# Hybrid block on one core: the first attention with 64-row score tiles, units of four pairs, decays from a 30-row matmul and no loop over batches

## The chip, the core and the metric

The kernel runs on one core of a Trainium2 chip, in one launch. The metric is the device time of that launch in microseconds (us). The engines are TensorE (PE; PEld is its weight load), VectorE (DVE), ScalarE (ACT), GpSimd (POOL) and SyncE (SP, which here only issues DMAs). Each runs its own instructions in order and waits on semaphores.

## The reference

Four layers stand behind one another, each behind a layernorm and with a residual: attention A, experts, a delta rule, experts. The change touches attention A alone, of which this is the core (8 batches B, T = 512 tokens, C = 128, 16 heads of 8):

```python
qkvgr = jnp.einsum('btc,oc->bto', x, W)
log_g = jax.nn.log_sigmoid(qkvgr[..., 3 * C:])
log_G = jnp.cumsum(log_g, axis=1).transpose(0, 2, 1)
S = jnp.einsum('bhtd,bhsd->bhts', Q, K)
Tm = DEG * jnp.log(jnp.abs(S) + EPS) + jnp.log(scale)      # DEG = 2
Z = Tm + log_G[..., :, None] - log_G[..., None, :]         # where s <= t
P = jnp.exp(Z - Z_rowmax)
y = (P @ V) / P.sum(-1)
```

So a weight is (|S| + eps)^2 times the decay exp(log_G[t] - log_G[s]), and the kernel computes it as that product, without the logarithm of S.

## The kernel before

Heads go in eight pairs p; a pair is 2Q + hf with Q in 0..3 and hf in 0..1. Tokens go in eight blocks of 64 (L = 64, index m). A batch is cut into 24 units (NU), 12 for each hf. Unit n has a key block m and the queries from block m on. For m < 4 it holds two pairs, for m >= 4 four pairs (`unit`, L134). Each unit goes through a line of engines:

- PE `scores` (L756): one matmul per pair. The weights `kf` are 128 rows by 128 columns with the two heads of the pair on the diagonal, 64 by 64 each, and zeros beside them. The moving operand is the bf16 feature tile `qf`. Rows are 48 products of three-part bf16 splits for each head.
- DVE `magnitude` (L577): the absolute value, from PSUM to SBUF.
- ACT `square` (L369): (|S| + eps)^2 into `pw`.
- POOL `diagonal` (L265): the diagonal block of the unit times `decay`, the masked decay inside a block.
- PE `attend` (L771): 64-column float32 matmuls with 18-column weights, one for each block and pair. The four Q write to four 32-partition groups of `pDia` and `pOff` and share the columns of the array.

PE is ahead by two units: at step n it issues `scores(n + 2)` and then `attend(n - 1)`. All engines run the same list of steps n = 0..23, with the preparation of the next batch put between the units at fixed n: TURN (transposes of the normalized x, n = 4), QK (projection, 6), the splits into bf16 parts (DVE, 8 and 10), VALUES (10), SUMS (15), DECAY (16 to 23, one m at each), EXPAND (18 and 20). `turn_back` and `finish` at n = 1 and 3 close the batch before.

The features go through HBM: SP writes the bf16 parts to `parts_scratch` by six DMAs (L168), waits for them, and loads `kc` (L173) and `qf` (L175), 1 MB each. DVE `expand` (L564) copies `kc` into the two diagonal halves of `kf`. For the decays POOL `ramps` (L237) makes tri times the log gate for each m, and PE `decay_sums` (L741) multiplies it by the 128-row float32 matrix `after` and adds the mask `never` by a bf16 matmul; ACT `decays` (L361) takes the exponential.

Batch 0 and the last batch are written out; batches 1 to 6 are a loop of three rounds on every engine (`Fori`, L187, L290, L426, L675, L852). Ahead of batch 0 stands a prologue: scaling of the weights with a guard from a POOL reduction (L231), the moments of all eight batches, and the preparation of batch 0.

## Time and profile before

| what | us |
|---|---|
| median of 3 runs | 1322.86 (1318.02 to 1323.44) |
| the profiled execution | 1334.64 |
| its span, first to last instruction | 1332.8 |
| attention A: start of the span to the last DVE instruction of the layer | about 502 |
| prologue: up to the first `attend` | 73.4 |
| batches 0 to 6, `attend` of one to that of the next | 391.8 in all |
| last batch to the last transpose | about 35 |

A row of a timeline begins with its start and its length in us. For PE a row is one group of like instructions; a float32 matmul of the program counts as two instructions. In brackets stands the idle time ahead of it and what ended it. The first `attend` of a batch begins with rows of L790 (the zero matmuls that start the accumulation), so these mark the batches: there are four such rows in each, two at n = 1 and 2, and two at n = 13 and 14.

### The profile page before, as it was taken

How to read it: one execution, taken by the hardware profiler on the slowest of the kernel's cores; microseconds unless marked ns; L12 is line 12 of the kernel's file. 1: busy time of each engine (PE TensorE's matmuls, PEld its weight loads, DVE VectorE, ACT ScalarE, POOL GpSimd, SP SyncE). 2: the span in 40 equal slices, each digit the busy share in tenths (PEclk: the TensorE clock that was granted, in tenths of full speed). 3: DMA queues.
4: the chain of work that ended last, by engine and by line, in shares of the span. 5: the costliest groups of instructions: out<-in, count | busy, mean ns of one | idle time of the engine just before them, and what ended most of it. 6: DMA issues, size and time to landing. Idle time of an engine off the chain costs nothing. (4 is left out here: it accounts for less than half of the span.)

```text
span 1332.8 us, 25209 instructions
## 1 busy us (share of the span) xinstructions
PE 912.9 (68%) x8236; PEld 629.3 (47%) x8236; DVE 793.4 (60%) x1615; ACT 551.8 (41%) x1205; POOL 578.7 (43%) x659
## 2 busy tenths in 40 slices
PE   0678878788787785029982958984676773507993
PEld 0355544545455462017771328734555563206772
DVE  6366676667676676202226129999999999501223
ACT  1465756566475652014431631015555541103441
POOL 3347467273655731444441000007777780172442
PEclk9989999899999996559995969996889887758997
DMA  2312303033040304036642680000001001016665
GB/s 69 126 65 65 128 3 128 18 112 112 19 128 7 122 3 192 32 96 181 185 137 76 205 205 1 1 0 0 0 0 63 16 16 32 9 52 164 183 188 166
DMA packets 129403, 110.08 MB, mean 83 GB/s; under 512 B 21984, under 2 KB 115104, under 8 KB 128928
## 3 DMA queue, kind: packets, MB, share of 16 engines
q1 hardware_dynamic: 123760, 98.08, 25.4%
q0 software_dynamic: 5120, 10.53, 2.4%
q8 instruction: 64, 1.05, 0.3%
q14 instruction: 27, 0.22, 0.1%
q10 hardware_dynamic: 432, 0.20, 0.1%
HBM read 64.01 MB, written 44.65 MB: 82 GB/s over the span
## 5 line engine op out<-in xcount | busy, mean ns | idle before, releaser
L583 DVE TENSOR_SCALAR a_mag<-a_pS 128x1024 int32<-128x1024 int32 (+1 forms) x192 | 182.1, 955 | 130.5 <-PE a_pS L767 128.7
L271 POOL TENSOR_TENSOR a_pw<-a_pw,a_decay 128x128 f32<-128x128 f32 (+1 forms) x192 | 121.3, 635 | 185.6 <-ACT a_pw L375 184.7
L375 ACT ACTIVATE a_pw<-a_mag,a_eps_a 128x1024 f32<-128x1024 f32 (+1 forms) x192 | 173.7, 928 | 64.7 <-DVE a_mag L583 63.8
L1053 POOL DMA_INDIRECT ys_dram<-f_yo,f_who x96 | 91.9, 957 | 139.3 <-DVE f_yo L1253 120.6
L1241 DVE TENSOR_SCALAR f_ysT<-f_bY,f_b2s 128x256 f32<-128x256 f32 x48 | 23.2, 484 | 175.1 <-PE f_bY L1341 147.3
L795 PE MATMUL a_pOff<-a_pw,a_vo 128*18 128x64 f32 x3584 | 126.5, 225 | 0.0
L1600 POOL TENSOR_TENSOR d_pb_p<-d_Q,d_s_sb 128x512 f32<-128x512 f32 x32 | 37.3, 1167 | 198.1 <-ACT d_s_sb L1700 198.1
L767 PE MATMUL a_pS<-a_qf,a_kf 128*128 128x128 bf16 (+7 forms) x512 | 98.4, 295 | 10.4 <-issue 6.8
L795 PEld LDWEIGHTS a_pOff<-a_pw,a_vo 128*18 128x18 f32 x3584 | 104.8, 102 | 0.0
L1096 ACT ACTIVATE f_hs<-f_bH,f_b1s 128x256 f32<-128x256 f32 x192 | 75.2, 474 | 67.1 <-issue 37.6
L1045 POOL DMA_INDIRECT xs_dram<-f_xa,f_pos x64 | 61.7, 964 | 94.0 <-DVE f_pos L1226 75.1
L2073 PE MATMUL d_c<-d_pb_p,d_ident 128*128 128x256 f32 x256 | 72.0, 450 | 43.4 <-POOL d_pb_p L1606 43.4
L1321 PE MATMUL f_bA<-ident,f_xs 128*128 128x128 f32 x96 | 21.6, 309 | 113.7 <-DMA f_xs<-xs_dram 62.8
L1331 PE MATMUL f_bH<-f_xsT,f_w1s 128*128 128x256 f32 x384 | 95.8, 394 | 0.0
L1341 PE MATMUL f_bY<-f_hs,f_w2s 128*128 128x256 f32 x384 | 90.8, 379 | 0.0
L243 POOL TENSOR_TENSOR a_ramp<-a_tri,a_logg 128x512 f32<-128x512 f32 x64 | 69.5, 1088 | 38.4 <-DVE a_logg L530 31.0
L2073 PEld LDWEIGHTS d_c<-d_pb_p,d_ident 128*128 128x128 f32 x256 | 58.2, 231 | 57.6 <-issue 42.2
L1087 ACT ACTIVATE f_xsT<-f_bA 128x256 f32<-128x256 f32 x48 | 18.4, 384 | 151.8 <-PE f_bA L1321 145.9
L750 PE MATMUL a_M<-a_ramp,a_after 128*128 128x512 f32 x128 | 73.8, 659 | 7.4 <-POOL a_ramp L243 6.8
L2073 PE MATMUL d_c<-d_pb_d,d_ident 128*128 128x256 f32 (+1 forms) x256 | 63.3, 413 | 22.0 <-POOL d_pb_d L1606 22.0
L1331 PEld LDWEIGHTS f_bH<-f_xsT,f_w1s 128*128 128x128 f32 x384 | 72.0, 197 | 9.6 <-issue 0.6
L792 PE MATMUL a_pDia<-a_pw,a_vd 128*18 128x64 f32 x1024 | 58.5, 228 | 25.0 <-POOL a_pw L271 24.4
(333 smaller groups left out, 1897.3 us busy)
## 6 DMA issues: line engine op xcount, KB each, us to landing
parts_scratch<-a_parts SPq DMA_DIRECT2D x32, 384.0 KB, 4.0
f_w1s<-in_L_ffn_w_dram SPq DMA_DIRECT2D x48, 256.0 KB
f_w2s<-in_L_ffn_w_dram SPq DMA_DIRECT2D x48, 256.0 KB
a_kc<-parts_scratch SPq DMA_DIRECT2D x8, 1024.0 KB, 6.0
a_qf<-parts_scratch SPq DMA_DIRECT2D x8, 1024.0 KB, 9.0
xs_dram<-blank SPq DMA_DIRECT2D x12, 516.0 KB, 5.3
f_xs<-xs_dram SPq DMA_DIRECT2D x48, 129.0 KB, 2.2
parts_scratch<-a_parts SPq DMA_DIRECT2D x16, 256.0 KB, 4.0
```

Of the source, the lines that this page charges most:

```text
L243: pool.tensor_tensor(ramp[:, m % 2, :, :], tri[:, :].unsqueeze(1).broadcast_to([P, NP, L]), logg[:, 0:64].rearrange("p (a m) -> p a m", m= ...
L271: pool.tensor_tensor(own, own, decay[:, k, m, pairs_of(hf, qs), :], ALU.mult)\
L375: act.activation(pw[:, n % 4, 0:N], mag[:, n % 3, 0:N], ACT.Square, bias=eps_a[:, 0:1])\
L583: dve.tensor_scalar(mag[:, n % 3, 0:2 * N].bitcast(I32).rearrange("p (l t) -> p l t", l=2), pS[:, 2 * (n % 2):2 * (n % 2) + 2, 0:N].bitcas ...
L750: pe.matmul(M[:, :], after[:, :], ramp[:, m % 2, :, :].rearrange("p a t -> p (a t)"), start=True, stop=False)
L767: ins = pe.matmul(pS[:, 2 * (n % 2) + l // half, at:at + width(m)], kf[:, k, p, m, :, :].rearrange("p x t -> p (x t)"), qf[:, k, p, L * m: ...
L795: ins = pe.matmul(pOff[lo:hi, L * i:L * i + L], vo[:, vo_at(m, i), p, :], wi, start=False, stop=(m == NM - 2), skip_group_check=True)
L1053: pool.indirect_dma_start(ys_dram[f][:, :], bass.IndirectOffsetOnAxis(ap=who[:, q, a:a + 1], axis=0), yo[:, q, a, :], None).then_inc(ys_ou ...
L1096: ins = act.activation(hs[:, q % 2, n, :], bH[:, 2 * (q % 2) + n // 2, ST * (n % 2):ST * (n % 2) + ST], ACT.Gelu, bias=b1s[:, q, n:n + 1])
L1331: ins = pe.matmul(bH[:, 2 * (q % 2) + n // 2, ST * (n % 2):ST * (n % 2) + ST], w1s[:, q, P * n:P * n + P], xsT[:, q % 2, :], start=True, s ...
L1341: ins = pe.matmul(bY[:, 0:ST], w2s[:, q, n, :], hs[:, q % 2, n, :], start=(n == 0), stop=(n == NF - 1))
L2073: ins = pe.matmul((c5, c6)[a][:, 0:64 * chunks].rearrange("p (c x) -> p c x", x=64), ident[:, :], po[:, k], start=(k == 0), stop=(k == 15))
```

## The change

Units: all 24 hold four pairs. For m < 4 the queries are cut in two instead of the pairs: a unit with the diagonal and one without (`BLOCKS`). The column counts of a unit are 4, 4, 4, 3, 3, 3, 3, 2, 4, 3, 2, 1 blocks of 64 for each pair.

Scores: each pair has two matmuls of 64 rows by 64 columns, one for each head, at rows and columns 0 to 63 and 64 to 127. `kf` is loaded directly in the form of `kc`, and `expand` and the zeros are gone. 64 score matmuls of a batch become 192.

Diagonals: POOL multiplies only in the 16 units of a batch that have a diagonal; `attend` of the other eight waits for ACT's `square` alone.

Decays: the ramps are gone. One more matmul at SUMS gives the cumulated log gates with the heads on partitions; DVE splits them in three bf16 parts (`cum_split`, n = 16); SP's `cumulated` writes them to HBM in two layouts, waits, and loads them into `here` and `there` (30 rows, with constants 1 and -1 in the other rows). A bf16 matmul of 30 rows gives a decay block. The eight decays of the next batch are done two at a time at n = 20 to 23.

The order: `Fori` is replaced by a Python loop on all engines. TURN 4 to 5, QK 6 to 7, VALUES 10 to 9 (with the second half of it behind the scores of n = 10), DECAY 16 to 20, `normalize` one batch earlier at n = 20, `finish` ahead of `magnitude`.

ACT: the natural logarithm and the exponential come from one table set, loaded once in the prologue.

Prologue: the moments of batch 0 alone are ahead of its normalization, those of batches 1 to 7 stand behind its splits; the guard's maximum goes over PE instead of POOL's reduction.

```diff
-        def width(m):
-            return T - L * m
+        BLOCKS = [part for m in range(NM) for part in
+                  ([(m, m, m + 4 - m // 2), (m, m + 4 - m // 2, NM)] if m < NM // 2 else [(m, m, NM)])]
         def unit(n):
             hf, r = divmod(n, HU)
-            if r < NM:
-                return hf, r // 2, (2 * (r % 2), 2 * (r % 2) + 1)
-            return hf, r - NM // 2, (0, 1, 2, 3)
+            return (hf,) + BLOCKS[r]
+        def on_diagonal(n):
+            return unit(n)[1] == unit(n)[2]
+        ND = sum(on_diagonal(n) for n in range(NU))
+        def diagonals(n):
+            return sum(on_diagonal(i) for i in range(n + 1))
...
-        TURN, QK, VALUES, SUMS, DECAY, EXPAND = 4, 6, 10, 15, 16, 18
+        TURN, QK, VALUES, SUMS, DECAY = 5, 7, 9, 15, 20
         FIN = (1, 3)
+        def decay_pair(n):
+            return (2 * n, 2 * n + 1) if 0 <= n < NM // 2 else ()
...
-                sp.wait_ge(s["kx_done"], 2 * bb)
-                sp.dma_start(kc[:, :, :], scratch[k, 1].rearrange("(p r) c t -> (r c) p t", p=NP))\
...
+            def cumulated(bb):
+                sp.wait_ge(s["cum_split"], 4 * bb + 4)
+                sp.wait_ge(s["cum_in"], 32 * bb)
+                sp.dma_start(cums[0].rearrange("q a m c -> (a m) q c"), cum3[:, :, :]).then_inc(s["cum_out"], 16)
+                sp.dma_start(cums[1].rearrange("q a m c -> q (a m c)").rearrange("q (x a m t) -> (a m) q x t", x=2, a=NP, m=NM),
+                             cum3[:, :, :].rearrange("p q (x t) -> p q x t", x=2)).then_inc(s["cum_out"], 16)
+                sp.wait_ge(s["cum_out"], 32 * bb + 32)
+                sp.wait_ge(s["decay_ps"], NM * bb)
+                sp.dma_start(here[6:KC, :, :], cums[0].rearrange("q a m c -> (q a) m c")).then_inc(s["cum_in"], 16)
+                sp.dma_start(there[0:6, :, :, :].rearrange("r a m t -> r (a m t)"),
+                             cums[1].rearrange("q a m c -> q (a m c)").rearrange("q (x f) -> (q x) f", x=2))\
+                    .then_inc(s["cum_in"], 16)
             features(0, 0)
+            sp.wait_ge(s["consts"], 2)
+            cumulated(0)
...
+                    cumulated(b + 1)
...
-            with sp.Fori(1, B - 2, 2) as b:
+            for b in range(1, B - 2, 2):
...
-            pool.wait_ge(s["guard_step"], 2)
-            pool.partition_all_reduce(wmx[:, :], wss[:, :], P, RMAX).then_inc(s["guard_step"], 1)
-            pool.wait_ge(s["guard_step"], 3)
-            for k in range(2):
-                pool.memset(kf[:, k, :, :, :, :].rearrange("p a m x t -> p (a m x t)").bitcast(F32), 0.0)\
-                    .then_inc(s["kf_zero"], 1)
-            def ramps(bb, m, first=False):
-                pool.wait_ge(s["logg_done"], bb + 1)
-                if not (first and m < 2):
-                    pool.wait_ge(s["decay_ps"], NM * bb + m - 1)
-                pool.tensor_tensor(ramp[:, m % 2, :, :],
-                                   tri[:, :].unsqueeze(1).broadcast_to([P, NP, L]),
-                                   logg[:, 0:64].rearrange("p (a m) -> p a m", m=NM)[:, :, m:m + 1]
-                                   .broadcast_to([P, NP, L]), ALU.mult).then_inc(s["ramp_done"], 1)
+            step(pool.memset(here[:, :, :], 0.0))
+            step(pool.memset(there[:, :, :, :], 0.0))
+            for q in range(3):
+                step(pool.affine_select(out=here[:, :, :].rearrange("p m (x t) -> p m x t", x=2),
+                                        in_=here[:, :, :].rearrange("p m (x t) -> p m x t", x=2),
+                                        compare_op=ALU.not_equal, fill=1.0, base=-2 * q,
+                                        pattern=[[0, NM], [-1, 2], [0, L]], channel_multiplier=1))
+                step(pool.affine_select(out=there[:, :, :, :].rearrange("p a m t -> p a (m t)"),
+                                        in_=there[:, :, :, :].rearrange("p a m t -> p a (m t)"),
+                                        compare_op=ALU.not_equal, fill=-1.0, base=-6 - NP * q,
+                                        pattern=[[-1, NP], [0, NM * L]], channel_multiplier=1))
+            pool.wait_ge(s["c_step"], st)
+            pool.sem_inc(s["consts"], 1)
...
-                    diagonal(b, n, k)
+                    if on_diagonal(n):
+                        diagonal(b, n, k)
...
+                    for m in decay_pair(n - DECAY - 1):
+                        decays(b + 1, 1 - k, m)
...
+            act.preload_act_table_set("natural_log_exp_and_others")
...
+            def cum_split(bb):
+                dve.wait_ge(s["cum_ps"], bb + 1)
+                dve.wait_ge(s["cum_out"], 32 * bb)
+                dve.tensor_copy(cum3[:, 0, :], M0[0:64, 192:320]).then_inc(s["cum_split"], 1)
+                dve.wait_ge(s["cum_split"], 4 * bb + 1)
+                dve.tensor_tensor(cum_r[:, :], M0[0:64, 192:320], cum3[:, 0, :], ALU.subtract)\
+                    .then_inc(s["cum_split"], 1)
+                dve.wait_ge(s["cum_split"], 4 * bb + 2)
+                dve.tensor_copy(cum3[:, 1, :], cum_r[:, :]).then_inc(s["cum_split"], 1)
+                dve.wait_ge(s["cum_split"], 4 * bb + 3)
+                dve.tensor_tensor(cum3[:, 2, :], cum_r[:, :], cum3[:, 1, :], ALU.subtract)\
+                    .then_inc(s["cum_split"], 1)
...
-            def expand(bb, k, par, first=False):
-                dve.wait_ge(s["feat_k"], 16 * bb + 16)
-                if first:
-                    dve.wait_ge(s["kf_zero"], 2)
-                else:
-                    dve.wait_ge(s["s_ps"], NU * (bb - 1))
-                lo, hi = L * par, L * par + L
-                dve.tensor_copy(kf[lo:hi, k, :, :, par, :].rearrange("p a m t -> p (a m) t"),
-                                kc[lo:hi, :, :].rearrange("p a (m t) -> p (a m) t", t=L))\
-                    .then_inc(s["kx_done"], 1)
...
+            dve.wait_ge(s["x_in"], 16 * (B - 1))
+            moments(1, B, 2 * TT)
             gate_prep(0)
+            rstds(1, B, 6)
...
+                    if n == 20 and b + 2 < B:
+                        normalize(b + 2)
+                    if n == QK + 1:
                         split_rest(b + 1, 0)
...
+            pe.wait_ge(s["guard_step"], 2)
+            pe.transpose(M1[0:2, 0:P], wss[:, :], ident[:, :]).then_inc(s["guard_step"], 1)
+            pe.wait_ge(s["guard_step"], 5)
+            pe.matmul(M1[:, P:P + 2], ones2[:, :], wmx2[:, :], start=True, stop=True).then_inc(s["guard_step"], 1)
...
+                pe.matmul(M0[0:64, 192:320], logg[:, 0:64], upto[:, :], start=True, stop=True)\
                     .then_inc(s["cum_ps"], 1)
             def decay_sums(bb, m):
-                pe.wait_ge(s["ramp_done"], NM * bb + m + 1)
+                pe.wait_ge(s["cum_in"], 32 * bb + 32)
                 if m >= 2:
                     pe.wait_ge(s["decay_sb"], NM * bb + m - 1)
                 if m == 1:
@@ -747,44 +791,49 @@
                     pe.wait_ge(s["cum_sb"], 6 * bb + 2)
                     pe.wait_ge(s["tok_ps"], bb + 1)
                 M = (M1, M0)[m % 2]
-                pe.matmul(M[:, :], after[:, :], ramp[:, m % 2, :, :].rearrange("p a t -> p (a t)"),
+                pe.matmul(M[:, :].rearrange("p (a t) -> p a t", t=L), here[:, m, :], there[:, :, m, :],
...
-                for l, Q in enumerate(qs):
+                for Q in range(4):
                     p = 2 * Q + hf
-                    half = len(qs) // 2
-                    at = width(m) * (l % half)
-                    ins = pe.matmul(pS[:, 2 * (n % 2) + l // half, at:at + width(m)], kf[:, k, p, m, :, :].rearrange("p x t -> p (x t)"),
-                                    qf[:, k, p, L * m:T], start=True, stop=True)
+                    at = L * (end - first) * (Q % 2)
+                    for par in range(2):
+                        lo, hi = L * par, L * par + L
+                        ins = pe.matmul(pS[lo:hi, 2 * (n % 2) + Q // 2, at:at + L * (end - first)],
+                                        kf[lo:hi, k, p, L * m:L * m + L], qf[lo:hi, k, p, L * first:L * end],
+                                        start=True, stop=True)
...
+                if first == m:
+                    pe.wait_ge(s["pdg_done"], ND * b + diagonals(n))
+                else:
+                    pe.wait_ge(s["sq_done"], NU * b + n + 1 + AHEAD_MAG)
...
+                        for m in decay_pair(n - DECAY):
+                            decay_sums(b + 1, m)
```

How the order moves at three places. First PE, around n = 19 to 21 of batch 0 before; `a_M` is the PSUM tile of the decays, `a_pS` that of the scores:

```order
L750 MATMUL a_M<-a_ramp,a_after 128x512
L752 MATMUL a_M<-a_never,a_ident_b 128x512
L767 MATMUL a_pS<-a_qf,a_kf 128x192 x4
L792 MATMUL a_pDia<-a_pw,a_vd 18x64 x2
L795 MATMUL a_pOff<-a_pw,a_vo 18x64 x8
L750 MATMUL a_M<-a_ramp,a_after 128x512
L752 MATMUL a_M<-a_never,a_ident_b 128x512
L767 MATMUL a_pS<-a_qf,a_kf 128x128 x4
L792 MATMUL a_pDia<-a_pw,a_vd 18x64 x2
L795 MATMUL a_pOff<-a_pw,a_vo 18x64 x8
```

The same steps of PE in the changed kernel:

```order
L812 MATMUL a_pS<-a_qf,a_kf 64x192 x8
L841 MATMUL a_pDia<-a_pw,a_vd 18x64 x4
L844 MATMUL a_pOff<-a_pw,a_vo 18x64 x8
L794 MATMUL a_M<-a_there,a_here 128x512
L796 MATMUL a_M<-a_never,a_ident_b 128x512
L794 MATMUL a_M<-a_there,a_here 128x512
L796 MATMUL a_M<-a_never,a_ident_b 128x512
L812 MATMUL a_pS<-a_qf,a_kf 64x128 x8
L844 MATMUL a_pOff<-a_pw,a_vo 18x64 x8
```

A decay stood in each step from n = 16 on; now two stand in each step from n = 20 on, ahead of that step's scores, and they read what SP's last two DMAs bring.

Second SP, the transfers of one batch before:

```order
L168 DMA parts_scratch<-a_parts 128x3x512 x2
L168 DMA parts_scratch<-a_parts 128x2x512
L168 DMA parts_scratch<-a_parts 128x3x512 x2
L168 DMA parts_scratch<-a_parts 128x2x512
L173 DMA a_kc<-parts_scratch 128x8x512
L175 DMA a_qf<-parts_scratch 128x8x512
```

And in the changed kernel:

```order
L180 DMA parts_scratch<-a_parts 128x3x512 x2
L180 DMA parts_scratch<-a_parts 128x2x512
L180 DMA parts_scratch<-a_parts 128x3x512 x2
L180 DMA parts_scratch<-a_parts 128x2x512
L184 DMA a_kf<-parts_scratch 128x8x512
L186 DMA a_qf<-parts_scratch 128x8x512
L193 DMA cum_scratch<-a_cum 64x3x128
L194 DMA cum_scratch<-a_cum 64x6x64
L198 DMA a_here<-cum_scratch 24x1024
L199 DMA a_there<-cum_scratch 6x4096
```

Four DMAs are new, and they stand behind the two large loads on the same queue.

Third DVE in the prologue, between the guard and the splits of batch 0, before:

```order
L456 TENSOR_SCALAR a_wn<-a_wn,a_guard 128x128
L458 COPY a_wT<-a_M 128x384
...
L470 BN_STATS a_stats<-x 128x6 x32
L474 BN_AGGR a_mv<-a_stats 128x2 x32
...
L496 TENSOR_SCALAR a_xn<-x,a_mv,a_rstd 128x128 x4
L504 TENSOR_TENSOR a_rest<-a_M,a_parts 128x512 x2
L510 TENSOR_TENSOR a_parts<-a_rest,a_parts 128x512 x2
L517 COPY a_gates<-a_M 128x4x8 x2
```

And in the changed kernel, where four statistics stand ahead of the guard:

```order
L513 TENSOR_SCALAR a_wn<-a_wn,a_guard 128x128
L521 TENSOR_SCALAR a_xn<-x,a_mv,a_rstd 128x128 x4
L648 COPY a_wT<-a_M 128x384
...
L529 TENSOR_TENSOR a_rest<-a_M,a_parts 128x512 x2
L535 TENSOR_TENSOR a_parts<-a_rest,a_parts 128x512 x2
L473 BN_STATS a_stats<-x 128x6 x28
L476 BN_AGGR a_mv<-a_stats 128x2 x28
...
L542 COPY a_gates<-a_M 128x4x8 x2
```

28 of the 32 statistics have moved from ahead of the normalization to between the splits and the gates.

## Rows read from the trace of the kernel before

**Rows 1.** Windows: stretch, length, busy us of PE, PEld, DVE, ACT, POOL, then PEclk.

```profile
410.80:435.40 24.60, 19.50 (x385) 13.45 (x385) 20.22 (x37) 15.28 (x23) 6.88 (x12) 1.00 0.13 41
435.40:465.20 29.80, 25.14 (x366) 14.45 (x368) 19.05 (x22) 19.40 (x28) 24.64 (x27) 1.00 0.35 111
465.20:500.00 34.80, 30.58 (x673) 21.74 (x672) 25.82 (x38) 20.52 (x25) 12.59 (x23) 0.95 0.01 3
```

**Rows 2.** Timeline of PE, the marks of batches 0, 6 and 7.

```profile
73.39 0.41 PE L790 MATMUL a_pOff<-a_pw,a_zeros 128*18 128x64 f32 x4 [3.87 <-POOL a_pw L271]
...
410.78 0.30 PE L790 MATMUL a_pOff<-a_pw,a_zeros 128*18 128x64 f32 x4
...
435.40 0.30 PE L790 MATMUL a_pOff<-a_pw,a_zeros 128*18 128x64 f32 x4 [2.00 <-issue]
...
465.17 0.30 PE L790 MATMUL a_pOff<-a_pw,a_zeros 128*18 128x64 f32 x4
```

**Rows 3.** Timeline of SP in batch 6.

```profile
431.67 4.64 SPq L168 DMA_DIRECT2D parts_scratch<-a_parts  x6
440.91 0.36 SPq L173 DMA_DIRECT2D a_kc<-parts_scratch  x1
441.31 0.58 SPq L175 DMA_DIRECT2D a_qf<-parts_scratch  x1
```

**Rows 4.** DMA view: count, KB each, median us from issue to landing.

```profile
a_kc<-parts_scratch SPq DMA_DIRECT2D x8, 1024.0 KB, 6.0
a_qf<-parts_scratch SPq DMA_DIRECT2D x8, 1024.0 KB, 9.0
...
f_xs<-xs_dram SPq DMA_DIRECT2D x48, 129.0 KB, 2.2
...
fg_dram<-d_pb_p SPq DMA_DIRECT2D x16, 32.0 KB, 2.7
```

**Rows 5.** Timeline of PE at n = 20 of batch 6.

```profile
449.95 1.13 PE L750 MATMUL a_M<-a_ramp,a_after 128*128 128x512 f32 x2
450.91 0.38 PE L752 MATMUL a_M<-a_never,a_ident_b 128*128 128x512 bf16 x1
451.13 0.39 PE L767 MATMUL a_pS<-a_qf,a_kf 128*128 128x128 bf16 x4
```

**Rows 6.** Timeline of PE, a unit of four pairs and the row after a unit of two.

```profile
401.10 0.52 PE L795 MATMUL a_pOff<-a_pw,a_vo 128*18 128x64 f32 x24
...
411.91 0.50 PE L767 MATMUL a_pS<-a_qf,a_kf 128*128 128x384 bf16 x2
```

**Rows 7.** Lines by form, 70 to 530 us: count, busy us, mean ns, idle before.

```profile
L271 POOL TENSOR_TENSOR a_pw<-a_pw,a_decay 128x128 f32<-128x128 f32 x128 | 68.3, 535 | 150.2 <-ACT a_pw L375 150.2
...
L243 POOL TENSOR_TENSOR a_ramp<-a_tri,a_logg 128x512 f32<-128x512 f32 x56 | 59.1, 1056 | 5.3 <-PE a_M L752 5.0 <-DVE a_logg L530 0.3
...
L271 POOL TENSOR_TENSOR a_pw<-a_pw,a_decay 128x256 f32<-128x256 f32 x64 | 53.0, 835 | 35.4 <-ACT a_pw L375 34.5
...
L573 DVE COPY a_kf<-a_kc 64x4096 bf16<-64x4096 bf16 x14 | 34.6, 2475 | 0.4
...
L353 ACT ACT_TABLE_LOAD x7 | 9.0, 1283 | 2.7 <-DVE a_tail L538 2.7
...
L538 DVE TENSOR_TENSOR a_tail<-a_b_tot,a_M 128x64 f32<-128x64 f32 x7 | 1.6, 222 | 0.2
```

**Rows 8.** Timeline of PE behind the loop's first back edge.

```profile
237.25 0.92 PE L767 MATMUL a_pS<-a_qf,a_kf 128*128 128x448 bf16 x2 [3.52 <-issue]
```

**Rows 9.** Timeline of the prologue, DVE, PE and SP.

```profile
18.74 2.61 DVE L456 TENSOR_SCALAR a_wn<-a_wn,a_guard 128x128 f32<-128x128 f32 x1
...
23.59 6.28 DVE L470 BATCH_NORM_STATS2 a_stats<-x 128x6 f32<-128x128 f32 x32
...
35.04 1.09 PE L703 MATMUL a_M<-a_ident,a_xn 128*128 128x128 f32 x4 [12.45 <-DVE a_xn L496]
...
43.44 4.65 SPq L168 DMA_DIRECT2D parts_scratch<-a_parts  x6
```

241 lines of the change are left out of this document (122 added, 119 removed).

## The prediction

> **What bounds the kernel now.** I read the marks of the batches in PE's timeline first [rows 2], then the windows between them [rows 1], and last the single rows of PE, SP and the lines by form. The reader is to see three things. First, the layer before the first attend takes 73.4 us, batches 0 to 6 take 465.17 - 73.39 = 391.8 us or 55.97 each, and the last one about 35 [rows 1, 2]. Second, in a batch without a loop's edge (batch 6, 54.4 us) PE is busy 19.50 + 25.14 = 44.6 us and DVE 39.3; PE idles a sixth and is the bound, with short stops in which a unit waits for DVE or POOL [rows 1]. Third, the last batch, which prepares no next one, takes 35: the preparation costs some 20 us of a batch, and the change works mostly on that.
>
> For the DMA chain I cut batch 6 into three parts by its marks [rows 2, 3, 5]: A, from the mark at n = 1 to the first DMA of the features, 431.67 - 410.78 = 20.9 us; B, from there to the decay of n = 20, 449.95 - 431.67 = 18.3; C, from there to the next mark, 465.17 - 449.95 = 15.2.
>
> **The change part by part.**
>
> Attend. A unit of two pairs with m = 0 takes from 410.78 to 411.91, 1.13 us for 36 instructions or 31 ns each; one of four pairs has its 24 of L795 in 0.52, the tail included, or 22 ns [rows 2, 6]. The units of m < 4 have 432 instructions in a batch (416 of L792 and L795, 16 of L790). PE saves 432 x 9.5 ns = 4.1 us.
>
> Scores. Twelve units of a half hold 4, 5, 2 and 1 groups of 256, 192, 128 and 64 columns for each pair. Four full-row matmuls of 128 columns take 0.31 us in the order of the queue (451.13 to 451.44, its length 0.39) [rows 5]; that is 78 ns for one against 53 ns of columns. I take the two 64-row matmuls of a pair as side by side, since the four Q of an attend already are. Then the sum of scores stays at some 10 us a batch. Bounds: it falls by nothing, and it rises by 10 us if they follow one another.
>
> Decays. The float32 pass takes 450.91 - 449.95 = 0.96 us, the bf16 mask 0.22 [rows 5]. The new matmul is bf16 with as many columns as the mask, so 0.22: 8 x 0.74 = 5.9 us less for PE. The extra matmul at SUMS is under 0.3.
>
> PE goes from 44.6 to about 44.6 - 4.1 - 5.9 + 0.3 = 34.9 us.
>
> DVE loses the two expansions, 2 x 2.475 = 4.95, and gains four operations of a size like L538's 0.222, together 0.9 [rows 7]: 39.3 - 4.1 = 35.2. ACT loses two table loads of 1.283 [rows 7]: 34.7 - 2.6 = 32.1. POOL loses 8 x 1.056 of ramps, and 16 x 0.535 of diagonals become 8 x 0.835 (68.3 us against 53.4 over all batches): 31.5 - 8.4 - 1.9 = 21.2 [rows 1, 7].
>
> With PE and DVE at 35 and units that hand over two deep, I would give a batch 42 us if nothing else bound it: the 35 of DVE and some 7 where one of the two has a step and the other waits (batch 6 has 10 of 54).
>
> The new wait. PE's decays of n = 20 need `here` and `there`. Behind the waiting PE instruction stand the scores of n = 20 on, so DVE, ACT and POOL run dry. The chain, from the first feature DMA t0: the load of `kf` is issued at t0 + 9.24, that of `qf` 0.40 later [rows 3]. `kf` lands 6.0 after its issue and `qf` 9.0 after its own [rows 4], that is 3.4 us apart though issued 0.4 apart: the one waits for the other on the queue. `qf` lands at t0 + 9.64 + 9.0 = 18.6. The two small writes are issued at t0 + 10.3, but stand behind 2 MB on the same queue; I give them 1 us behind `qf`, 19.6. Then SP issues the two reads (0.4 each) and they land as a small load does, 2.2 [rows 4]: 22.5. The bounds of this: if the writes were not held back, they would land 2.7 after their issue [rows 4], and the whole would be t0 + 16; reads that share the engines with `qf` make 18.5 of it. If writes of 128 and 256 bytes a piece take 2 us more, 24.5. Without a wait PE would come to n = 20 about 13 us after t0 (nine units of 1.5, less the first). So B is set by the wait: 22.5, taken because the landing times of `kc` and `qf` are the nearest rows.
>
> A, after: DVE has in it its magnitudes, finish, splits and gates, which are now later by one step (n = 11 instead of 10) but without a wait for an old turn. DVE was busy 20.2 of 24.6 in the first half [rows 1]. I take 20 (18 to 22). C, after: PE has five units less 8 x 0.74 of work, but ACT has eight exponentials there in four units, and POOL the seven products of `vo`; part of those is done during the wait. PE comes out of an idle time of 22.5 - 13 = 9.5 us, and after the idle 3.5 of the loop's edge two matmuls of 448 columns took 0.92 us [rows 8]; their columns alone are 0.75 at 1.2 GHz and 0.37 at 2.4, so PE came back at the lower clock. Unslowed, C's PE work is some 9 us by the rows above (eight decays at 0.43, five groups of scores and of attends at 0.4 to 0.5, a turn back under 1), with ACT's exponentials beside it 10; I take 12 (10 to 15). A batch: 20 + 22.5 + 12 = 54.5, seven of them 381.5, against 391.8: -10.3. That includes the loop's edges: two in batches 2 and 4, 3.5 us each with a slow clock behind them [rows 8]. Code that is written out has to be fetched too; the written-out batches 0 and 7 show no such stop.
>
> Prologue. DVE no longer does all statistics ahead of the first transposes: 6.28 us and as much as is left to 35.04 [rows 9], and the guard no longer waits for POOL. The scaling of the weights took 2.61 us at 18.74, while POOL filled `kf`. The transposes start at 35.04. From 23.59 on lie 11.4 us of statistics, their deviations and the normalization, of which some 10 go; the scaling's 2.3 above its usual 0.3 go; and the guard, which began behind POOL's reduction and POOL's fill, comes an estimated 9 earlier: near 13.5. POOL now fills and selects `here` and `there` in the same stretch, 4096 elements a row like `kf`; if each of DVE's operations is held as that one was, it is 21. I take 17. From there to the first attend: 38.4 before; now 8.4 to the features' first DMA [rows 9], the 22.5 of the chain, eight decays that PE and ACT hand to each other at about 0.95, and 4 us for one unit's magnitude, square, diagonal and handovers (estimates): 42.5. So 59.5 instead of 73.4: -14 (-10 to -19).
>
> Last batch: two-pair units gone, 4.1 us of PE, of which DVE (25.8 of 34.8 busy) lets through some 3: -3.
>
> Sum: -14 - 10 - 3 = -27 against the profiled execution's 1334.64, whose span is 1332.8: 1307.6. The median of the runs is 11.8 lower than that execution: 1296.
>
> **The rivals.**
>
> The wait is shorter. The small writes pass the large loads, or land with them. For it: they are only 48 KB each and the write side is idle. Against: the two loads landed one after the other. B is 18.5, and C loses 1.5 since the idle time is short: 7 x -5.5 = -38.5, 1257.
>
> No wait at all. The units are slower than I think, or the chain is faster, so that n = 20 comes later. Then a batch is 42: 7 x -12.5 = -87.5, 1208. Against it: the old kernel itself reached n = 20 18.3 us after t0, 4 us before the 22.5.
>
> Slower: the clock. After each wait of 10 us PE runs at 1.2 GHz, and if it stays there through C and into A, because units with waits between them do not raise it again, C's 9 us of PE work doubles to 18, A becomes 21 and B, with the slow small writes, 24: 63 a batch, 7 x 8.5 = +59.5, 1355. It decides from 58.4 us a batch on, where 1323 is reached. For it: [rows 8]. Against: at 465 the clock is 0.95 over a batch with short stops [rows 1].
>
> The score halves follow one another. The two matmuls of a pair write two halves of one PSUM bank. If that holds the second back, scores double by 10 us a batch; 15 of 24 units lie outside B, and DVE covers a quarter: 7 x 4.8 = +33.6, 1330, at the edge of no change. Against: the four Q of attend write four groups of one bank and take 22 ns each [rows 6]. The Trainium skill, page TensorEngine Tiling (Array Packing), section Restrictions and Gotchas, says that different row tiles cannot use the same PSUM bank at once; attend's groups are column tiles, so no row here speaks against that rule. By it the time would be the 1330 of this paragraph.
>
> **How the numbers follow.** The forecast 0.45; wait shorter 0.20; no wait 0.10; the clock 0.13; the halves 0.12. The forecast's own range, from A, B, C and the prologue, is 1268 to 1322. For the whole I leave out most of no wait and the upper part of the clock: 1228 to 1336. A measurement here can tell about 0.5% from no change, 1316.2 to 1329.5. Faster: 0.42 of the forecast, 0.30 of the two shorter cases and 0.01 of the halves, 0.73. Same: 0.03 of the forecast, 0.06 of the halves, 0.02 of the clock, 0.11. Slower: 0.05 of the halves and 0.11 of the clock, 0.16.
>
> **What would show it.** In the changed profile: the row of L794 at n = 20 with several us of idle ahead of it, ended by a DMA into `here` or `there`; marks of the batches (L839) 54 us apart; a first mark near 60; L812 groups of 8 matmuls of 256 columns near 0.5 us, or near 1 if the halves follow one another; PE busy about 35 us in a batch; a granted clock under 0.95 in the stretches behind the wait. It would be wrong if the decays find their data in time, if the marks lie under 48 or over 59 us apart, or if the first mark is over 66.

## The result, and the profile after

The changed kernel is slower: a median of 1341.66 us against 1323.15 of the kernel before beside it, a ratio of 1.013 (95% interval 1.0078 to 1.0181). One of its runs was disturbed and is out of that ratio. The profiled execution took 1342.41 us with a span of 1340.6. The forecast was 1296, its range 1228 to 1336.

Where the time went, first by windows. These three answer to [rows 1]: batch 6 up to n = 13, from there to the next mark, and the last batch (same columns; PEclk is the seventh number, behind POOL's).

```profile
428.46:450.76 22.30, 17.32 (x449) 12.19 (x449) 18.64 (x33) 15.67 (x23) 5.82 (x8) 1.00 0.05 16
450.76:485.70 34.94, 25.00 (x422) 13.68 (x423) 14.99 (x25) 16.96 (x26) 13.98 (x15) 0.66 0.36 119
485.70:522.00 36.30, 25.09 (x776) 18.06 (x776) 28.72 (x51) 21.14 (x25) 12.20 (x19) 0.91 0.02 3
```

The first half of a batch is 2.3 us shorter, the second 5.1 longer, with the granted clock at 0.66 where it was 1.00. PE is busy 25.00 of the 34.94 us there, at that clock; DVE, ACT and POOL are busy under half.

The marks in PE's timeline answer to [rows 2].

```profile
69.48 0.31 PE L839 MATMUL a_pOff<-a_pw,a_zeros 128*18 128x64 f32 x7 [0.54 <-POOL a_pw L291]
...
428.46 0.31 PE L839 MATMUL a_pOff<-a_pw,a_zeros 128*18 128x64 f32 x7 [0.48 <-ACT a_off_sb L400]
...
450.76 0.44 PE L839 MATMUL a_pOff<-a_pw,a_zeros 128*18 128x64 f32 x8 [2.46 <-issue]
...
485.70 0.31 PE L839 MATMUL a_pOff<-a_pw,a_zeros 128*18 128x64 f32 x7 [0.48 <-ACT a_off_sb L400]
```

The prologue is 69.5 us (before 73.4), batches 0 to 6 are 485.70 - 69.48 = 416.2 (before 391.8), and the last one, to DVE's first instruction of the experts at 520.46, 34.8 (before 502.82 - 465.17 = 37.7). That is -3.9, +24.4 and -2.9, together +17.6; the medians say +18.5. The rest of the kernel has the same code; it took 820.1 us in this execution and 830.0 in the profiled one of before, which is why the two profiled executions differ by 7.8 only.

SP's timeline in batch 6 answers to [rows 3], the landing times to [rows 4].

```profile
449.01 4.47 SPq L180 DMA_DIRECT2D parts_scratch<-a_parts  x6
457.63 0.36 SPq L184 DMA_DIRECT2D a_kf<-parts_scratch  x1
458.03 0.58 SPq L186 DMA_DIRECT2D a_qf<-parts_scratch  x1
458.92 1.24 SPq L193 DMA_DIRECT2D cum_scratch<-a_cum  x1
460.19 0.88 SPq L194 DMA_DIRECT2D cum_scratch<-a_cum  x1
466.65 0.32 SPq L198 DMA_DIRECT2D a_here<-cum_scratch  x1
467.01 0.30 SPq L199 DMA_DIRECT2D a_there<-cum_scratch  x1
```

```profile
a_kf<-parts_scratch SPq DMA_DIRECT2D x8, 1024.0 KB, 6.1
a_qf<-parts_scratch SPq DMA_DIRECT2D x8, 1024.0 KB, 8.6
```

PE at n = 20 answers to [rows 5]:

```profile
469.56 0.60 PE L794 MATMUL a_M<-a_there,a_here 30*128 30x512 bf16 x1 [7.73 <-DMA a_there<-cum_scratch]
470.10 0.61 PE L796 MATMUL a_M<-a_never,a_ident_b 128*128 128x512 bf16 x1
470.64 0.60 PE L794 MATMUL a_M<-a_there,a_here 30*128 30x512 bf16 x1
```

The wait is there, 6.5 to 9.2 us in each batch. The matmuls of the decays behind it begin 0.54 us apart up to 481.3, where they are 0.32 apart at a clock of 1.00 (e13 below); eight decays and what stands between them fill C without a stop, up to the 0.48 ahead of the mark. The windows around the wait, in order of time:

```profile
454.11:460.94 6.83, 5.15 (x150) 3.56 (x149) 5.31 (x13) 3.28 (x5) 1.61 (x2) 1.00 0.48 159
460.94:461.83 0.89, 0.84 (x24) 0.59 (x24) 0.67 (x2) 0.52 (x1) 0.00 (x0) 0.50 1.06 377
461.83:469.56 7.73, 0.01 (x1) 0.00 (x0) 1.69 (x2) 2.08 (x3) 6.34 (x5) 0.50 0.58 189
469.56:481.42 11.86, 11.86 (x111) 4.46 (x111) 2.34 (x3) 5.40 (x9) 4.17 (x5) 0.50 0.01 1
```

Two things are to be seen. The clock fell 0.9 us before the long wait began, behind three short stops of PE (0.21, 0.59 and 0.93 us for DVE and POOL); it did so in batches 1, 3, 4 and 6, and at the beginning of the wait or within it in 5, 0 and 2. And it stayed at 0.50 for 11.86 us in which PE never stopped; in the seven batches it came back 10.6 to 18.2 us behind the wait. Cut by the marks as in the prediction, the means over seven batches are A 21.5, B 20.7, C 17.2, in all 59.5.

### The profile page after: what moved, and what is told of

It is laid out like the page before. It is cut to its first block and busy times, and to the rows that moved or that the text cites. A ratio compares the mean times of both kernels' runs of the same rounds, so it can differ in the third digit from the quotient of the medians.

```text
span 1340.6 us, 25894 instructions
## 1 busy us (share of the span) xinstructions
PE 888.5 (66%) x9215; PEld 615.8 (46%) x9215; DVE 773.1 (58%) x1639; ACT 535.4 (40%) x1190; POOL 498.4 (37%) x529
## 5 line engine op out<-in xcount | busy, mean ns | idle before, releaser
L608 DVE TENSOR_SCALAR a_mag<-a_pS 128x1024 int32<-128x1024 int32 (+1 forms) x192 | 178.7, 951 | 179.3 <-PE a_pS L812 177.5
L291 POOL TENSOR_TENSOR a_pw<-a_pw,a_decay 128x256 f32<-128x256 f32 x128 | 95.8, 752 | 259.2 <-ACT a_pw L392 259.0
L812 PE MATMUL a_pS<-a_qf,a_kf 64*64 64x192 bf16 (+3 forms) x1536 | 116.0, 279 | 10.8 <-DVE a_mag L608 10.1
L844 PE MATMUL a_pOff<-a_pw,a_vo 128*18 128x64 f32 x3584 | 98.0, 246 | 0.0
L279 POOL TENSOR_TENSOR a_vo<-a_vd,a_reach 128x1008 f32<-128x1008 f32 (+6 forms) x56 | 66.2, 1186 | 67.7 <-ACT a_reach L374 34.2
L812 PEld LDWEIGHTS a_pS<-a_qf,a_kf 64*64 64x64 bf16 x1536 | 66.7, 119 | 53.6 <-DVE a_mag L608 24.2
L2122 PEld LDWEIGHTS d_c<-d_pb_p,d_ident 128*128 128x128 f32 x256 | 58.3, 231 | 60.1 <-issue 45.0
L794 PE MATMUL a_M<-a_there,a_here 30*128 30x512 bf16 x64 | 37.7, 590 | 64.2 <-DMA a_there<-cum_scratch 64.2
L844 PEld LDWEIGHTS a_pOff<-a_pw,a_vo 128*18 128x18 f32 x3584 | 70.7, 112 | 10.7 <-issue 6.3
L1136 ACT ACTIVATE f_xsT<-f_bA 128x256 f32<-128x256 f32 x48 | 18.5, 385 | 142.9 <-PE f_bA L1370 137.2
L2122 PE MATMUL d_c<-d_pb_d,d_ident 128*128 128x256 f32 (+1 forms) x256 | 60.7, 400 | 21.6 <-POOL d_pb_d L1655 21.6
```

The costliest lines, as they stand in the source:

```text
L279: pool.tensor_tensor(vo[:, vo_at(j, j + 1):vo_at(j, j + 1) + n, :, :], vd[:, k, j, :, :].unsqueeze(1).broadcast_to([P, n, NP, 18]), reach[ ...
L291: pool.tensor_tensor(own, own, decay[:, k, m, hf:NP:2, :], ALU.mult)\
L608: dve.tensor_scalar(mag[:, n % 3, 0:2 * N].bitcast(I32).rearrange("p (l t) -> p l t", l=2), pS[:, 2 * (n % 2):2 * (n % 2) + 2, 0:N].bitcas ...
L812: ins = pe.matmul(pS[lo:hi, 2 * (n % 2) + Q // 2, at:at + L * (end - first)], kf[lo:hi, k, p, L * m:L * m + L], qf[lo:hi, k, p, L * first: ...
L844: ins = pe.matmul(pOff[lo:hi, L * i:L * i + L], vo[:, vo_at(m, i), p, :], wi, start=False, stop=(m == NM - 2), skip_group_check=True)
L2122: ins = pe.matmul((c5, c6)[a][:, 0:64 * chunks].rearrange("p (c x) -> p c x", x=64), ident[:, :], po[:, k], start=(k == 0), stop=(k == 15))
```

## The experiments

Each group of kernels (e1 to e4, e5 to e8, e9 to e12, e13 and e14) ran beside the kernel before on one chip. That kernel's median was 1333.1, 1322.8, 1334.2 and 1322.9 us in the four groups, so the ratios are what to compare; the changed kernel's is 1.013. "Filling" stands for idle matmuls whose result nobody reads. e1 and e6 use the decays of batch 0 for all batches: they price the wait and are no versions to keep. In the edits below operands are shortened. First mark, batch (mean of 0 to 6), A, B and C are read in the profiles, in us.

| kernel | ratio (interval) | first mark | batch | A | B | C |
|---|---|---|---|---|---|---|
| before | 1 | 73.4 | 56.0 | | | |
| changed | 1.013 (1.008 to 1.018) | 69.5 | 59.5 | 21.5 | 20.7 | 17.2 |
| e1_nocum | 0.972 (0.969 to 0.974) | 69.5 | 51.2 | 20.6 | 12.5 | 18.0 |
| e2_filler | 0.992 (0.989 to 0.995) | 69.6 | 55.7 | 20.9 | 21.0 | 13.8 |
| e3_ramps | 0.961 (0.959 to 0.964) | 53.7 | 51.2 | | | |
| e4_lateconst | 1.005 (1.003 to 1.007) | 57.5 | 59.4 | 21.0 | 20.6 | 17.8 |
| e5_actq | 1.010 (1.007 to 1.012) | 69.5 | 58.3 | 20.8 | 20.5 | 17.0 |
| e6_nocum_fill | 0.962 (0.960 to 0.963) | 69.5 | 49.5 | 21.6 | 15.0 | 12.9 |
| e7_ramps_fill | 0.935 (0.933 to 0.936) | 54.2 | 46.8 | | | |
| e8_unrolled | 0.992 (0.991 to 0.994) | 72.1 | 54.5 | | | |
| e9_cumfirst | 0.989 (0.987 to 0.991) | 69.7 | 54.6 | 21.0 | 15.9 | 17.7 |
| e10_values | 0.946 (0.944 to 0.948) | 54.4 | 48.3 | | | |
| e11_mended | 0.993 (0.991 to 0.996) | 57.6 | 57.5 | 19.4 | 21.0 | 17.1 |
| e12_stops | 0.937 (0.935 to 0.939) | 54.6 | 46.9 | | | |
| e13_mended44 | 0.967 (0.963 to 0.971) | 57.3 | 52.1 | 19.6 | 21.1 | 11.4 |
| e14_stops3 | 0.951 (0.948 to 0.955) | 54.5 | 50.0 | | | |

**e1_nocum: the wait away.**

```diff
-                    cumulated(b + 1)
-                pe.wait_ge(s["cum_in"], 32 * bb + 32)
+                pe.wait_ge(s["cum_in"], 32)
```

> The changed kernel without the four small DMAs of batches 1 to 7: the decays of these batches use what batch 0 loaded into here and there, so the output is not the reference's; DVE's split and all of PE's decay matmuls stay. Theory (the wait and the slow clock behind it): the 8.3 us of idle ahead of the decays of n = 20 go in every batch, and so does the stretch at clock 0.50 behind them, in which C (decay of n = 20 to the next mark) took 17.2 instead of the 12 forecast. Then n = 20 comes some 13 us after the first feature DMA, and scores of n = 22, which need qf, wait until 18.6 after it: 21.5 + 18.6 + 6 = 46 to 48 us a batch instead of 59.5, and 1342 - 7 x 12 = 1258 (1245 to 1272). Rival (the batch is bound by something else, the queue of the DMAs is only where it shows): batches stay over 55 us and the time over 1310. Rival (only the wait goes, the clock stays low since other stops lower it too): 51 us a batch, 1283.

The wait is gone, and B is 12.5. C is not shorter. This window is C of batch 4, from its first decay to the mark at 325.42:

```profile
307.20:325.42 18.22, 17.54 (x177) 7.78 (x169) 12.02 (x13) 11.57 (x17) 11.56 (x12) 0.53 0.17 59
```

PE is busy 17.54 of 18.22 us at clock 0.53. So the second rival holds, with its 51 us a batch: the wait costs 8 us of B, and the slow clock in C doesn't need it. Ahead of C PE had stopped 2.46 us at n = 13, then 0.21, 0.60 and 0.92 for DVE and POOL, as in the changed kernel.

**e2_filler: the wait kept and filled.**

```diff
+                        if n == DECAY:
+                            for _ in range(30):
+                                pe.matmul(M1, ident_b, never, start=True, stop=True)
                         for m in decay_pair(n - DECAY):
```

> The changed kernel with 30 bf16 matmuls of 512 columns more at n = 20 of batches 0 to 6, ahead of the wait for here and there, their result overwritten by the decay. They are 30 x 0.22 = 6.6 us of PE at full clock and fit in the idle 6.5 to 9.2 us. Theory (PE comes out of the idle time at the lower clock and this costs 5 us of C): the granted clock stays at 1.00 or comes back within C, decays take 0.22 each instead of 0.54, C falls from 17.2 to about 12 us, and the time by 7 x 5 = 35 to 1307 although 46 us of work are added. Rival (C is bound by ACT and POOL, whose eight exponentials and seven products stand there): the clock is high and C still 16 to 17, time within 1335 to 1345. Rival (the matmuls run at half clock, since the idle time begins earlier): they take 13 us, the wait is overrun by 5 us, time 1375 or more.

Two batches in PE's timeline, the filling and the first decay behind it:

```profile
269.87 6.65 PE L889 MATMUL a_M<-a_never,a_ident_b 128*128 128x512 bf16 x30
279.21 0.39 PE L794 MATMUL a_M<-a_there,a_here 30*128 30x512 bf16 x1 [2.69 <-DMA a_there<-cum_scratch]
...
327.74 6.65 PE L889 MATMUL a_M<-a_never,a_ident_b 128*128 128x512 bf16 x30
334.84 0.39 PE L794 MATMUL a_M<-a_there,a_here 30*128 30x512 bf16 x1 [0.46 <-DMA a_there<-cum_scratch]
```

46 us of useless work make the kernel 2% faster, some 28 us where I had expected 35. In batches 0 to 6 the rest of the wait was 0, 2.29, 1.35, 2.69, 0.46, 2.06 and 1.10 us, and C was 11.4, 16.7, 11.4, 15.5, 11.4, 16.4 and 14.2. C at clock 1.00 is 11.4, near the 12 that I forecast for it; its excess is the clock, which fell again in batches 1, 3, 5 and 6. ACT and POOL do not bind it.

**e11_mended and e13_mended44: is that all of it?** Both are the changed kernel with a filling of n = 20 (30 and 44 matmuls), POOL's constants behind the normalization (e4), eight filling matmuls at n = 13 and the values behind the attend of n = 9 (e7). The edit between the two:

```diff
-                            for _ in range(30):
+                            for _ in range(44):
```

> The changed kernel, its decay part kept, with four edits: 30 idle matmuls ahead of the wait of n = 20 (e2), POOL's constants behind the normalization (e4), eight idle matmuls ahead of the attend of n = 13 and the values behind the attend of n = 9 (e7). Theory (clock and POOL's fills were the whole of what the change lost beyond the wait): first mark at 57.5, A 19.7 and B 20.7 as the wait sets them, C 11.4 at clock 1.00, a batch 51.8; against the changed kernel 12 + 7 x 7.7 = 66 us less, ratio to before 0.963 (0.955 to 0.975); so the decay part still costs 5 us a batch against e7_ramps_fill. Rival (the clock falls in some of the batches all the same, as in batches 1, 3 and 5 of e2): 54 to 55 a batch, ratio 0.98.

> The kernel of e11_mended with 44 idle matmuls ahead of the wait of n = 20 instead of 30. In e2_filler the batches whose rest of the wait was 0, 1.35 and 0.46 us had C in 11.4, those with 2.29, 2.69 and 2.06 had 15.5 to 16.7; in e11_mended all seven rests were 2.7 to 3.9 and C 16.1 to 17.8. Theory (what is left of the stop decides C's clock): 14 more matmuls are 3.1 us, the rest falls under 1 us in all batches, C is 11.4, A 19.7, B 20.7, a batch 52, and the ratio to before 0.963 (0.955 to 0.972), with 22 us of work more than in e11_mended. Rival (another stop, or the decays themselves, lower the clock): C stays 16 to 18, ratio 0.99 or more.

e11 missed: the rest of the wait was 2.7 to 3.9 us in all batches, since PE, at full clock up to there, came to n = 20 earlier. The clock fell in all seven. With 44, the rests are 0 to 0.9 and C is 11.35 or 11.36 in every batch. C of batch 6 in e11, then in e13:

```profile
442.63:460.16 17.53, 17.53 (x169) 7.65 (x169) 5.62 (x7) 9.39 (x14) 5.30 (x7) 0.53 0.00 1
```

```profile
410.80:422.15 11.35, 10.91 (x168) 5.65 (x169) 5.39 (x7) 8.41 (x14) 5.23 (x7) 1.00 0.01 3
```

The same instructions take PE 17.53 us at 0.53, without any stop, and 10.91 at 1.00. 14 matmuls more in a batch, 22 us of work, are worth 2.6% of the time. What is left against e7 below, 5.3 us a batch, I put down to the wait; e6 below, with these decays and no wait, has 49.5, and its A is 2.0 longer than that of e13.

**e3_ramps: the decay part undone, the rest kept.**

```diff
-        TURN, QK, VALUES, SUMS, DECAY = 5, 7, 9, 15, 20
+        TURN, QK, VALUES, SUMS, DECAY = 5, 7, 9, 15, 16
...
-                pe.wait_ge(s["cum_in"], 32 * bb + 32)
+                pe.wait_ge(s["ramp_done"], NM * bb + m + 1)
-                pe.matmul(M, here[:, m, :], there[:, :, m, :], start=True, stop=False)
+                pe.matmul(M, after[:, :], ramp[:, m % 2, :, :], start=True, stop=False)
```

> The changed kernel with the decay part undone: POOL makes the ramps (eight of 1.06 us a batch), PE's decays are the float32 matmul with after and stand one at each step from n = 16, no here, there, cum_split or small DMA, and POOL fills no constants of 4096 elements a row in the prologue. Units of four pairs, 64-row tiles, the order of the rest and the written-out batches stay. Theory (the decay part alone turned a gain into a loss): PE has 40.5 us of work in a batch, DVE 34.4, no wait over 3 us at n = 20, clock 0.95 or more, a batch is 49 to 51, the first mark comes at 60 to 65, and the time is 1342 - 7 x 9.5 - 7 = 1268 (1255 to 1285). Rival (units of four pairs, 64-row tiles or the unrolled code cost as much themselves): over 1310.

As the theory has it, 3.9% faster than before where the whole change is 1.3% slower. The batch came at 51.2, just above its 49 to 51, and the first mark at 53.7, below its 60 to 65. The clock missed its 0.95: it is 0.83 to 0.93 over a batch, falling at the stops ahead of the values and at n = 13, which e7 and e10 take up. PE's own sizes at clock 1.00 stand in the lines by form of one batch, of before (batch 6) and of e7 (batch 5), which shares the units and tiles:

```profile
L795 PE MATMUL a_pOff<-a_pw,a_vo 128*18 128x64 f32 x448 | 15.0, 219 | 0.0
...
L792 PE MATMUL a_pDia<-a_pw,a_vd 128*18 128x64 f32 x128 | 7.2, 224 | 3.8 <-POOL a_pw L271 3.7
```

```profile
L808 PE MATMUL a_pOff<-a_pw,a_vo 128*18 128x64 f32 x448 | 10.4, 220 | 0.0
...
L805 PE MATMUL a_pDia<-a_pw,a_vd 128*18 128x64 f32 x128 | 4.9, 225 | 1.4 <-POOL a_pw L272 1.4
```

Attend falls from 22.2 to 15.3 us, more than the 4.1 I gave it. The score lines of the same two views sum to 12.4 and 12.6: unchanged.

**e4_lateconst: POOL's constants later.**

```diff
+            pool.wait_ge(s["xn_done"], TT)
             step(pool.memset(here[:, :, :], 0.0))
```

> The changed kernel in which POOL begins to fill and select here and there only once the normalized x of batch 0 is there. Theory (in the prologue POOL's fills and selects hold DVE: L500 took 3.50 us, L484 3.28, L493 3.56, L513 3.33, each of which works on a few hundred elements): these operations fall under 0.4 us, the first transposes of x start near 17 instead of 27.2, and the first mark comes 3 to 9 us earlier, since a part is given back where the fills now hold the splits and moments; time 1333 to 1339. Rival (DVE waits there for something else, such as the load of x): transposes stay at 27 and the time at 1342.

DVE and PE in the prologue of the changed kernel, then of e4:

```profile
7.22 3.51 POOL L255 MEMSET a_there<- 30x4096 bf16 x1
...
7.26 3.50 DVE L500 TENSOR_SCALAR a_wmx<-a_ident,a_wmx 2x2 f32<-2x2 f32 x1
...
17.65 3.33 DVE L513 TENSOR_SCALAR a_wn<-a_wn,a_guard 128x128 f32<-128x128 f32 x1
...
20.90 5.27 DVE L521 TENSOR_SCALAR a_xn<-x,a_mv,a_rstd 128x128 f32<-128x128 f32 x4
...
27.18 1.11 PE L746 MATMUL a_M<-a_ident,a_xn 128*128 128x128 f32 x4 [5.03 <-DVE a_wvg L654]
```

```profile
7.05 0.22 DVE L501 TENSOR_SCALAR a_wmx<-a_ident,a_wmx 2x2 f32<-2x2 f32 x1
...
9.38 0.28 DVE L514 TENSOR_SCALAR a_wn<-a_wn,a_guard 128x128 f32<-128x128 f32 x1
9.57 1.11 DVE L522 TENSOR_SCALAR a_xn<-x,a_mv,a_rstd 128x128 f32<-128x128 f32 x4
...
11.97 1.12 PE L747 MATMUL a_M<-a_ident,a_xn 128*128 128x128 f32 x4 [1.14 <-DVE a_wvg L655]
```

An operation on 2 by 2 numbers took 3.50 us while POOL filled 4096 elements a row, and 0.22 without it. The transposes come 15.2 us earlier; 3.2 of that is lost again where the fills now meet the splits, and the first mark is 12.0 earlier, more than expected. The Trainium skill, page Trainium Architecture — The Big Picture, section What this means for kernel authors, says that DVE and GpSimd share a port pair under an exclusive lock; the two views agree, 3.50 against 0.22.

**e5_actq and e9_cumfirst: what makes the small writes late.** In e5 ACT issues the four small DMAs on its queue; in e9 SP issues them ahead of the loads.

```diff
+            def cum_write(bb):
+                act.wait_ge(s["cum_split"], 4 * bb + 4)
+                act.dma_start(cums[0].rearrange("q a m c -> (a m) q c"), cum3[:, :, :]).then_inc(s["cum_out"], 16)
...
                         token_decay(b + 1, 1 - k)
+                        cum_write(b + 1)
+                    if n == SUMS + 3:
+                        cum_read(b + 1)
```

```diff
                 sp.wait_ge(s["parts_out"], 96 * bb + 96)
+                if bb:
+                    cumulated(bb)
                 sp.dma_start(kf[:, k, :, :], scratch[k, 1]...
```

> The changed kernel with the four small DMAs issued by ACT on its own queue: the two writes at n = 17 behind the exponential of the token decays, the two reads at n = 18. Theory (the small writes are held back by the 2 MB of kf and qf ahead of them on SP's queue, 5.5 to 6.5 us a batch): they land 2 to 3 us after their issue, the reads 2 to 3 us later, and the decay of n = 20 comes 15 to 16.5 us after the first feature DMA instead of 20.7; seven times -4.5 and the prologue's unchanged: -31 against the changed kernel, ratio to before 0.990 (0.98 to 1.00), C still 17 to 18 at the lower clock. Rival (the 16 DMA engines are full with the 2 MB, whichever queue asks): writes land with qf, B stays over 19.5, ratio 1.005 to 1.02. Rival (ACT, which now waits for the writes at n = 18, holds up its squares, which the reads on SP did not): B over 20 with PE waiting for ACT or DVE ahead of n = 20.

> The changed kernel in which SP issues the four small DMAs of a batch ahead of the loads of kf and qf instead of behind them (batch 0 as before). In e5_actq the small writes took 7 us on ACT's queue as they did on SP's, with the 2 MB under way in both. Theory (they wait for the DMA engines, which the two large loads fill, whichever queue they are on): with the engines free the writes land some 2.7 after their issue, the reads 2.2 after theirs, and the decay of n = 20 comes 15 to 16 us after the first feature DMA instead of 20.7; kf and qf are issued 4 to 5 us later, so qf lands at 23 and the scores of n = 22 wait for it a little. B + C is 33 to 35 instead of 37.9, and the ratio to before 0.990 to 1.000. Rival (small DMAs of this shape take 6 us by themselves): B stays 19 to 21, the features come later still, ratio 1.03.

ACT's timeline in e5, the first write and the first read; then SP's in e9; then the DMA views of the changed kernel, e5 and e9 (KB each, median us from issue to landing):

```profile
334.47 0.62 ACTq L364 DMA_DIRECT2D cum_scratch<-a_cum  x1
...
341.91 0.30 ACTq L371 DMA_DIRECT2D a_here<-cum_scratch  x1
```

```profile
210.27 0.59 SPq L195 DMA_DIRECT2D cum_scratch<-a_cum  x1
...
213.46 0.32 SPq L200 DMA_DIRECT2D a_here<-cum_scratch  x1
```

```profile
cum_scratch<-a_cum SPq DMA_DIRECT2D x16, 48.0 KB, 6.5
...
cum_scratch<-a_cum ACTq DMA_DIRECT2D x16, 48.0 KB, 6.7
...
cum_scratch<-a_cum SPq DMA_DIRECT2D x16, 48.0 KB, 2.1
```

From the first write to the read that waits for both it is 7.4 us on the other queue, 7.7 on SP's behind the loads (458.92 to 466.65), and 3.2 ahead of them. In e5 ACT idles 5.9 us there, ended by the landing of the writes, so it is they that take the time and not ACT's own order. So the theory of e5 fell and that of e9 holds: the writes wait for the 2 MB under way, not for their place in a queue. The Trainium skill, page DMA: Bandwidth & Descriptors, section Queues, rings and completion order, says that each engine takes turns between queues packet by packet; by it I would have expected the writes to come through sooner on ACT's queue, and these rows show 0.3 us of it. e9 gains 2.4% on the changed kernel by order alone, with C still slow.

**e6_nocum_fill, e7_ramps_fill, e10_values: the short stops.**

```diff
+                    if n in (17, 18, 19) and not last:
+                        spend(M1, 3)                       # e6: ahead of and behind the scores
...
+                    if n == HU + 1 and not last:
+                        spend(M0, 8)                       # e7: ahead of the attend of n = 13
...
-                        if n == VALUES:
-                            values(b + 1)                  # e7, e10: from ahead of the scores
+                    if n == VALUES and not last:
+                        values(b + 1)                      # to behind the attend
```

> The kernel of e1_nocum (no small DMAs behind batch 0) with 18 matmuls of 512 bf16 columns more in a batch, three ahead of and three behind the scores of n = 17, 18 and 19; their results are never read. They are 4.0 us at full clock. In e1_nocum PE stopped there 0.21, 0.60 and 0.92 us, and C ran at clock 0.53 in 18.2 us although no wait for a DMA stood ahead. Theory (C's length is the clock alone, and short stops of PE at n = 17 to 19 are enough to lower it): C is 11.4 to 12 us at clock 1.00, B 13 to 15, a batch 46 to 48 with perhaps a short wait for qf at n = 22, and the time 7 x 4 below that of e1_nocum, ratio to before 0.951 (0.945 to 0.96). Rival (the clock falls in C for another reason, such as the decays' own matmuls): C stays 18 and the batch is 53, ratio 0.985.

> The kernel of e3_ramps with two edits against PE's stops: eight matmuls of 512 bf16 columns more (1.8 us, never read) ahead of the attend of n = 13, where PE waits 2.46 us for the copies of pOff and pDia, and the values behind the scores and the attend of n = 9 instead of ahead of them, where PE waited 1.79 us for DVE. Theory: the rows behind the stop of n = 13 run at full clock (0.52 instead of 0.85 for eight scores of 192 columns), which gives 2 us a batch, the other edit gives 1: 48 a batch instead of 51.2, ratio to before 0.946 (0.94 to 0.955). Rival (these rows are not on the path, DVE is): 51 a batch, ratio 0.96.

> The kernel of e3_ramps with one of the two edits of e7_ramps_fill: the values behind the scores and the attend of n = 9; no added matmuls. Theory (most of e7's gain is the clock that no longer falls at the two stops, and either stop alone lowers it for the rows behind): the stop of 2.46 us at n = 13 stays with some 3 us at the lower clock behind it; a batch is 48.5 to 50 against 51.2 (e3) and 46.7 (e7), ratio to before 0.950 (0.943 to 0.957). Rival (the values' place did all): 46.7 to 47.5, ratio 0.937. Rival (it did nothing, the added matmuls did all): 51, ratio 0.961.

In e6 C fell from 18.0 to 12.9, B grew by 2.5, and A by 1.0, since in four of seven batches the clock now fell in A (22 to 23 us instead of 20.6); the ratio is 0.962 for the 0.951 expected. C's clock is 1.00 in batches 1 to 6, without the wait and with the short stops filled; what it has above 11.4 in batches 1 to 5 is a stop of 1.34 us, in which PE waits for the exponential of a decay. In e7 the clock is 1.00 in both halves of batches 1 to 6; this is batch 6:

```profile
335.04:356.44 21.40, 19.11 (x458) 12.88 (x457) 18.45 (x33) 14.99 (x23) 5.80 (x8) 1.00 0.05 17
356.44:381.78 25.34, 23.11 (x428) 12.60 (x429) 15.09 (x21) 17.22 (x26) 21.84 (x23) 1.00 0.46 157
```

46.8 us a batch against 51.2 in e3; I had expected 48. e10, with the values' place alone, has 48.3, within its 48.5 to 50 but for 0.2. So of e7's gain over e3 about two thirds come from the values' place, which also takes PE's stop there from 1.79 to 0.98, and a third from filling n = 13. e7 is the fastest version: 1236.7 us, 6.5% under the kernel before.

**e12_stops and e14_stops3: stops put into e7.**

```diff
+                    if n in (18, 19) and not last:
+                        pe.wait_ge(s["mag_done"], NU * b + n + 4)     # e12
+                    if n in (19, 20, 21) and not last:
+                        pe.wait_ge(s["sq_done"], NU * b + n + 5)      # e14
```

> The kernel of e7_ramps_fill with two stops put in: at n = 18 and 19 PE's scores wait for the magnitude of the unit before (one further than they need), which is 0.5 to 1.5 us each. No work is added. Theory (two short stops within a few us let the clock fall, and what they cost is the slow stretch, not themselves): behind them the granted clock is 0.50 to the end of the batch, the decays take 1.9 us instead of 0.96, and a batch takes 53 to 56 instead of 46.7, ratio to before 0.97 to 0.985. Rival (only the stops' own length is lost): 47.5 to 49.5 a batch at clock 0.95 or more, ratio 0.94 to 0.95.

> The kernel of e7_ramps_fill with stops at n = 19, 20 and 21 of batches 0 to 6: PE's scores of that step wait until ACT's square of the unit before theirs is done, which needs the scores, the magnitude and the square of that unit one after the other. No work is added. In e12_stops the waits put in were met already, and it took what e7 took. Here each should stop PE 0.7 to 1.5 us. Theory (short stops close together lower the clock of a batch that has no other wait): the granted clock falls to 0.50 behind them, a float32 decay takes 1.9 us there, and the batch grows by the stops' 3 us and 3 to 6 us of slow matmuls, to 53 to 55 from 46.7; ratio to before 0.966 to 0.985. Rival (three stops of about 1 us are too short): 49 to 50 at clock 1.00, ratio 0.947 to 0.953.

e12 says nothing: the waits were met already. e14 does, and against me. PE's timeline and the window around:

```profile
389.48 0.52 PE L776 MATMUL a_pS<-a_qf,a_kf 64*64 64x192 bf16 x8 [1.72 <-ACT a_pw L376]
...
393.24 0.41 PE L776 MATMUL a_pS<-a_qf,a_kf 64*64 64x128 bf16 x8 [1.51 <-ACT a_pw L376]
...
396.56 0.31 PE L776 MATMUL a_pS<-a_qf,a_kf 64*64 64x64 bf16 x8 [1.30 <-ACT a_pw L376]
```

```profile
381.00:401.00 20.00, 15.47 (x249) 7.35 (x249) 8.32 (x10) 9.85 (x16) 17.15 (x17) 1.00 0.34 114
```

Three stops of 1.3 to 1.7 us, with two of work between them, left the clock at 1.00 in batches 1 to 6; only the stops' own time was lost (49.6 a batch), as the rival has it. In batch 0 the same three stops did lower it: it is 0.87 from the decay on, and the batch took 52.5. In e1 shorter ones (0.21, 0.60, 0.92) came within 3.4 us, and it fell; in e13 the same three stand with little change ahead of the filling, and it did not. Which set of stops lowers it stays open.

**e8_unrolled: the loop alone.**

```diff
-            with sp.Fori(1, B - 2, 2) as b:
+            for b in range(1, B - 2, 2):
```

> The kernel before with batches 1 to 6 written out on all five engines instead of the loop of three rounds, and nothing else. Theory (the loop's edges cost what the trace of before shows, two idle times of 3.5 us with matmuls at the lower clock behind them, in batches 2 and 4, which took 58.3 and 57.9 against 54.4): 6 to 10 us are gained, ratio 0.994 (0.992 to 0.997). Rival (code written out costs as much in fetching): ratio 1.000 or more.

0.8% faster, at the far end of the theory. Four of the six batches of the former loop take 54.3, the others 55.8 and 55.3.

## Why the prediction was wrong

**The step that failed is C.** "Unslowed, C's PE work is some 9 us ...; I take 12 (10 to 15)." It measured 17.2, and 7 x 5.2 = 36 us is most of the miss. The work was sized nearly right. With the clock at 1.00 C is 11.4, with 10.9 of PE in it for the 9 (e13), and a batch has 47.3 us of PE there, 9.7 and 1.9 of them filling, so 35.7 for the 34.9. What failed is that PE would be back at full clock soon behind the wait: the clock stayed at 0.50 for 10.6 to 18.2 us, though PE did not stop. What I had as a rival of 0.13, "if it stays there through C", is what happens, and the row that bears it, [rows 8], was in front of me. I set against it that before ran at 0.95 over short stops. That compared a full PE with one that the change had just lightened.

**The rival's mechanism is half right.** It gave A 21, B 24, C 18, and a batch of 63; measured are 21.5, 20.7, 17.2, and 59.5, just past its point of decision at 58.4. But it blamed the wait of 10 us alone. e1 has no wait, and C is 18.0; and in four batches of the changed kernel itself the clock fell before the wait began. PE stops there for DVE and POOL; e6 fills these stops and has C at 12.9. That this is because PE has less to do beside a DVE with four operations more is my reading; no run takes these away. The Trainium skill, page TensorE: Matmul & The Clock Gate, section HAM oscillation — how this bites in real kernels, describes a PE that falls to half clock at each wait for a DMA and starts the next burst slow. The trace agrees (0.54 us for 512 columns behind the wait, 0.32 in e13), and e1 adds that a wait for a DMA is not needed.

**A: 21.5 for 20.** The same again. In batches 0 to 4 the clock fell at the stop of 1.79 us ahead of the values and A was 21.5 to 22.2; in 5 and 6 it did not and A was 20.6. With the values behind the attend the stop is 0.98 and A 19.6 (e13). 7 x 1.5 = 11 us.

**B: 20.7 for 22.5.** Chain and order were right. The writes took 7.7 us for the 9.3 I gave them, the reads the 2.9 that I gave, from their issue to the decay. That gave 13 us back. Without the wait PE comes to n = 20 12.5 us after the first feature DMA (e1), for my 13. The reason was wrong in part: the small writes wait for the engines, not for their queue (e5, e9).

**Prologue: -3.9 for -14.** I took the first transposes at 17 (21 if every operation were held); they came at 27.2. Of DVE's operations there four took 3.3 to 3.6 us, and the normalization 5.3 for 1.1. Without the fills it is 12.0 and the first mark 57.5, under my 59.5 (e4). Only the fills' price was too small, by 10 us.

**Attend, scores, decays, last batch.** Attend was sized at -4.1 and is about -7 of PE's busy time. Scores are unchanged: the halves run side by side. In the first half of batch 6:

```profile
443.18 0.62 PE L812 MATMUL a_pS<-a_qf,a_kf 64*64 64x256 bf16 x8
443.73 0.72 PE L763 MATMUL a_M<-a_wvg,a_xnT 128*64 128x72 f32 x16
```

Eight matmuls of 256 columns take 0.55 us to the next row's start, 69 ns each, where the columns of one are 107 at 2.4 GHz. That rival is out (its price was also 4.7 a batch by its own terms, 10 x 15/24 x 3/4, not 4.8), and with it, for this kernel, the rule of the page TensorEngine Tiling (Array Packing) of the Trainium skill, section Restrictions and Gotchas: here two row tiles do write halves of one bank at once. A decay is 0.64 at clock 1.00 (0.32 a matmul in e13) against 1.18 before [rows 5], so -4.3 a batch for the -5.9 I took from the mask's 0.22. These two misses go against each other, which is luck. The last batch is -2.9 for -3.

**The sum.** Prologue +10, A +11, B -13, C +36: +44 on a forecast of 1296 is 1340, and 1342 was measured. The one judgement that turned the sign was that PE returns to full clock by itself soon behind the wait: with C at 12 the kernel would have come out near 1305.

## What to carry to other kernels

Where a change makes TensorE's work shorter, or puts a wait into its stream, price the matmuls behind each of its stops at half clock as well, and look whether the gain survives; if it doesn't, idle matmuls into a free tile before the awaited one are cheap to try (30 a batch alone gave 2%, the step from 30 to 44 in e13 2.6%). Look for what shares a resource with a new step, not only for what waits on it: POOL's fills held DVE, and 2 MB of loads held 96 KB of writes. Test the parts of a bundle one by one: here the parts other than the decays were worth 3.9% of the time before, and the decays with their wait and constants lost 5.2% of it.

## What of the hardware was not expected

- Useless matmuls made a kernel faster: 30 a batch by 2%, the step from 30 to 44 by 2.6%.
- A PE that does not stop stayed at the lower clock for long: 17.53 us busy of 17.53 at 0.53 (e11), 11.86 of 11.86 at 0.50 (the changed kernel).
- In the prologue DVE operations on SBUF took as long as the POOL fill or select beside them (3.50 us for 2 by 2 elements), while BATCH_NORM_STATS2 did not: 28 took 5.50 us in e4 beside POOL's selects and 5.50 in the changed kernel without them.
- Small writes took 7.4 us beside 2 MB of loads on another queue and 3.2 with the engines free.
- The decay's two matmuls of 512 columns, which alternate, are 0.32 us apart at clock 1.00; the same mask matmul repeated is 0.22 (6.65 for 30). No run tells why.
- The rest of the kernel, whose code is the same everywhere, goes by the chip: 830 to 835 us in the profiled executions of e1 to e4 and e9 to e12, where the kernel before has a median of 1333 and 1334, and 816 to 821 in those of e5 to e8, e13 and e14, where it has 1323. Two profiled executions from different chips can so differ by 10 us without any change.
